# Graph network on one core: entering rows as two f32r halves, turned and summed in one matmul

## The reference

```python
x = layernorm(x + L0(x, adj))     # 5 groups of at most 25 nodes, two graph convolutions each, rows 0..24 alone change
x = layernorm(x + L1(x, adj, mask))
# L1:
A = (adj != 0)
h = x
for l in range(5):
    m = h @ weight[l]
    agg = A^T m                    # per graph, 128 x 128
    h = gru(agg, h)                # r, z: sigmoid of sums of two products; n: tanh(i_n + r * h_n)
return h * mask
```

## Time and profile before

| what | us |
|---|---|
| median of 3 runs (534.69 to 535.28) | 534.74 |
| profiled execution, its own time | 534.39 |
| its span, first to last instruction | 532.1 |
| TensorE busy | 514.9 |
| VectorE busy | 437.5 |
| ScalarE busy | 369.4 |
| GpSimd busy | 249.3 |

### The profile page before, as it was taken

One profiled execution on the slowest core, in us unless ns is written; L12 is line 12 of the kernel. 1 busy time (PEld: TensorE's weight loads), 2 busy tenths in 40 slices (PEclk: granted clock), 3 DMA queues, 4 the chain that ended last, 5 costly groups with the idle time before them and its releaser, 6 DMA issues.

```text
span 532.1 us, 8535 instructions
## 1 busy us (share of the span) xinstructions
PE 514.9 (97%) x2993; PEld 441.2 (83%) x2993; DVE 437.5 (82%) x970; ACT 369.4 (69%) x683; POOL 249.3 (47%) x299
## 2 busy tenths in 40 slices
PE   7999999999999999999999999999999999999991
PEld 6888889888888889888888889888888888888870
DVE  5479775899979877889979986688988998877886
ACT  2468665767876676787786676787785678786645
POOL 7569422458532354457633254546552245332334
PEclk9999999999999999999999999999999999999995
DMA  5967610000000000000000000000000000010002
GB/s 138 220 181 178 165 34 4 1 1 0 2 1 0 9 25 22 21 20 22 1 1 1 1 0 22 22 20 21 0 2 1 1 1 20 25 37 0 1 0 79
DMA packets 35579, 17.29 MB, mean 32 GB/s; under 512 B 4321, under 2 KB 35498, under 8 KB 35538
## 3 DMA queue, kind: packets, MB, share of 16 engines
q1 hardware_dynamic: 32233, 14.99, 10.7%
q10 hardware_dynamic: 2665, 1.54, 1.0%
q0 software_dynamic: 640, 0.22, 0.3%
HBM read 12.54 MB, written 4.19 MB: 31 GB/s over the span
## 4 chain that ended last, share of the span: by engine, by line
PE 92%; DVE 3%; SPq 2%; DMA 1%; ACT 1%; POOL 1%; issue 0%; DVEq 0%; POOLq 0%
PE p L1260 20%; PE p L1262 20%; PE p L1261 20%; PE p L1254 13%; PE p L1247 8%; PE p L1138 3%; PE p L1112 1%; PE p L1131 1%; PE p L1121 1%; DMA xt<-in_x_dram 1%; SPq L273 1%; PE p L1176 1%; SPq L268 1%; PE p L1168 1%; DVE st L930 0%; PE p L1063 0%
## 5 line engine op out<-in xcount | busy, mean ns | idle before, releaser
L486 POOL TENSOR_TENSOR dg<-hT,ng 128x512 f32<-128x512 f32 x80 | 126.1, 1576 | 255.7 <-ACT ng L706 255.6
L1260 PE MATMUL p<-ghi,wf 128*128 128x512 f32 x240 | 101.1, 421 | 0.0
L1260 PE MATMUL p<-hhi,wh 128*128 128x512 f32 x237 | 99.6, 420 | 0.0
L1262 PE MATMUL p<-ghi,wf 128*128 128x512 f32 x240 | 94.4, 393 | 0.0
L1261 PE MATMUL p<-glo,wf 128*128 128x512 f32 x240 | 93.6, 390 | 0.0
L1262 PE MATMUL p<-hhi,wh 128*128 128x512 f32 x237 | 93.1, 393 | 0.0
L1261 PE MATMUL p<-hlo,wh 128*128 128x512 f32 x237 | 92.5, 390 | 0.0
L1010 DVE SCALAR_TENSOR_TENSOR cg<-p,biasc,rg 128x512 f32<-128x512 f32 x80 | 59.9, 748 | 37.8 <-ACT rg L688 36.8
L688 ACT ACTIVATE rg<-p,gb 128x512 f32<-128x512 f32 x80 | 55.4, 692 | 34.8 <-PE p L1262 29.0
L706 ACT ACTIVATE ng<-cg,biasc 128x512 f32<-128x512 f32 x80 | 57.9, 724 | 23.1 <-DVE cg L1013 22.7
L1254 PEld LDWEIGHTS p<-an,nat 128*128 128x128 f32 x512 | 66.9, 191 | 5.1
(11 more groups left out here) (157 smaller groups left out, 846.9 us busy)
## 6 DMA issues: line engine op xcount, KB each, us to landing
xn<-in_x_dram SPq DMA_DIRECT2D x8, 512.0 KB, 4.8
an<-in_adj_dram SPq DMA_DIRECT2D x8, 512.0 KB, 7.4
out_dram<-xn SPq DMA_DIRECT2D x15, 256.0 KB, 2.3
xt<-in_x_dram SPq DMA_DIRECT2D x16, 50.0 KB
w<-in_L_gnn_W_dram ACTq DMA_DIRECT2D x1, 640.0 KB, 5.8
w<-in_L_gnn_W_dram SPq DMA_DIRECT2D x1, 640.0 KB, 4.4
zg<-in_L_gnn_weight_dram ACTq DMA_DIRECT2D x1, 320.0 KB, 3.9
xt<-in_x_dram SPq DMA_DIRECT2D x8, 36.0 KB
```

What stands on the lines that cost most here:

```text
L486: nc.gpsimd.tensor_tensor(dg[:, w.k % 2, :], hT[:, w.slot, :], ng[:, w.k % 2, :], ALU.subtract).then_inc(d_ok, 1)
L1260: MM(bank[:], w[:, 0, cols], xhi, start=start, stop=False)
L1262: return MM(bank[:], w[:, 1, cols], xhi, start=False, stop=stop)
```

## The change

- The rows of an entering visit are split into two f32r halves in er (two buffers, by visit parity): the high half by a copy (VectorE at the end of window i = 17 for the chunk's visits 0 and 1, ScalarE in windows k = 19, 20 and so on for visits 2 and 3), the low half by a subtraction on GpSimd in the window in which the visit enters, ahead of that window's dg.
- enter_and_aggregate takes the place of the four transposes and the f32 sum: per graph two f32r matmuls, weights the high and the low rows, moving 256 columns: the graph's ones and an identity that stands behind them as an's 65th block. The result holds, per graph, the masked sums and the turned state side by side; the four graphs fill banks PG and PL.
- So the entering state is there only at the end of window k. ScalarE copies the sums' high half ahead of tanh. In window k+1 it waits for glo, makes hhi, waits for the low half, and copies hT; all this stands ahead of nat and r. VectorE makes the low half (lo_entering) first of all in window k+1, ahead of the leaving rows.
- The adjacency is loaded to a buffer raw of one chunk and goes from there, as ones, to an (now f32r). SP loads a chunk's raw once the chunk before is through.
- The transposes of L0's adjacency stand at the end of window i = 2 for every chunk, and their scaling at the start of window i = 3. The neighbours' matmuls go behind the turn.
- ghi, glo have 2 buffers, nat has one.

```diff
+        er = sb("er", [128, 2, 2, SB, D], f32r)
+        both = PGL[:].rearrange("p (q o n) -> p q o n", q=SB, o=2)
+        SUMS, STATE = both[:, :, 0, :], both[:, :, 1, :]
...
+            def enter_and_aggregate(k):
+                visit = ALL_WINDOWS[k].enter
+                for q in range(SB):
+                    b = visit * SB + q
+                    moving = an[:, b:B + 1:B - b, :]
+                    MM(both[:, q], er[:, visit % 2, 0, q, :], moving, start=True, stop=False)
+                    last = MM(both[:, q], er[:, visit % 2, 1, q, :], moving, start=False, stop=True)
+                last.then_inc(G_ps, 1)
...
@@ ScalarE, window k
-                    if w.i == adjacency_in(c):
+                    if w.i == Plan.Y:
                         adjacency(c)
...
+                if coming_in(k - 1) is not None:
+                    high_state(coming_in(k - 1), None)
+                    if coming_in(k - 1) % SLOTS < 2:
+                        high_rows(coming_in(k - 1) + 2)
+                    state(coming_in(k - 1), None)
                 if w.out == "step":
                     act.wait_ge(T_ps, w.turned + 1)
...
-                if w.enter is not None and k >= 2:
-                    state(w.enter, PL)
-                    high_state(w.enter, PL)
...
+                if coming_in(k) is not None:
+                    aggregated(k + 2, None)
                 act.wait_ge(c_ok, k + 1)
@@ state and high_state, visits from 4 on
+                    act.wait_ge(glo_ok, first_window(visit) + 1)
+                    nc.scalar.copy(by_graph(hhi[:, visit % SLOTS, :]), STATE).then_inc(hi_ok, 1)
...
+                    act.wait_ge(lo_ok, first_window(visit) + 1)
+                    nc.scalar.copy(by_graph(hT[:, visit % SLOTS, :]), STATE).then_inc(hT_ok, 1)
@@ VectorE
+            def lo_entering(m):
+                dve.wait_ge(hi_ok, made(m))
+                TT(by_graph(hlo[:, m % SLOTS, :]), STATE, by_graph(hhi[:, m % SLOTS, :]), ALU.subtract).then_inc(lo_ok, 1)
+            def high_rows(visit):
+                dve.wait_ge(ln1_ok, visit + 1)
+                dve.wait_ge(G_ps, first_window(visit) - 2)
+                nc.vector.tensor_copy(er[:, visit % 2, 0], xn[:, visit * SB:(visit + 1) * SB, :]).then_inc(ehi_ok, 1)
...
-                if k >= 2 and w.enter is not None:
-                    lo_state(k + 2)
@@ GpSimd, ahead of dg in window k
+                if coming_in(w.k) is not None:
+                    low_rows(w.k)
@@ TensorE
-                if w.enter is not None and k >= 2:
-                    pe.wait_ge(ob_ok, (NG - 1) * (w.enter // SLOTS + 1))
-                    pe.wait_ge(hi_ok, k + 2)
-                    pe.wait_ge(hT_ok, w.enter)
-                    enter(w.enter, PL)
+                if c is not None and w.i == Plan.Y:
+                    neighbours(c)
...
+                if c is not None and w.i == Plan.Y - 1:
+                    pe.wait_ge(hT_ok, SLOTS * c)
+                    pe.wait_ge(lo_ok, k + 2)
+                    if c > 1:
+                        pe.wait_ge(x_ok, 2 * PACK * (c - 1))
+                    adjacency(c)
```

More of the change, by code:

```diff
@@ L143, in build @@
         xn = sb("xn", [128, B, D])
-        an = sb("an", [128, B, N])
+        an = sb("an", [128, B + 1, N], f32r)
+        raw = sb("raw", [128, CB, N])
         hT = sb("hT", [128, SLOTS, COLS])
@@ L147, in build @@
         hlo = sb("hlo", [128, SLOTS, COLS], f32r)
-        nat = sb("nat", [128, SLOTS, SB, D])
-        ghi = sb("ghi", [128, SLOTS, COLS], f32r)
-        glo = sb("glo", [128, SLOTS, COLS], f32r)
+        nat = sb("nat", [128, SB, D])
+        er = sb("er", [128, 2, 2, SB, D], f32r)
+        ghi = sb("ghi", [128, 2, COLS], f32r)
+        glo = sb("glo", [128, 2, COLS], f32r)
         rg = sb("rg", [128, 2, COLS])
@@ L210, in build, with by_graph @@
         rs2, nm2 = sb("rs2", [128, SLOTS, SB]), sb("nm2", [128, SLOTS, SB])
-        P = [ctx.enter_context(nc.psum_tensor(f"p{i}", [128, 512], f32)) for i in range(8)]
+        P = [ctx.enter_context(nc.psum_tensor(f"p{i}", [128, 512], f32)) for i in range(5)]
+        PGL = ctx.enter_context(nc.psum_tensor("pgl", [128, 2 * 512], f32))
+        P += [PGL[:, 0:512], PGL[:, 512:1024]]
+        P.append(ctx.enter_context(nc.psum_tensor("p7", [128, 512], f32)))
         PR, PH, PZ, PI, PT, PG, PL, PM = P
+        both = PGL[:].rearrange("p (q o n) -> p q o n", q=SB, o=2)
+        SUMS, STATE = both[:, :, 0, :], both[:, :, 1, :]
+        def by_graph(ap):
+            return ap.rearrange("p (q n) -> p q n", q=SB)
         WF_BANKS = (3, 4, 6, 0, 3)
@@ L283, in load_chunk, with load_graphs @@
         def load_chunk(eng, c):
-            for dst, src in ((xn, x), (an, adj)):
-                for b in (c * CB, c * CB + CB // 2):
-                    load_half(eng, dst, src, b, xa_in)
+            for b in (c * CB, c * CB + CB // 2):
+                load_half(eng, xn, x, b, xa_in)
+        def load_graphs(eng, c):
+            for at in (0, CB // 2):
+                load_half(eng, raw, adj, c * CB + at, raw_in, at)
         def group_cols(g):
@@ L330, in _ @@
                 load_half(sp, xn, x, h * CB // 2, x0_in[h])
-                load_half(sp, an, adj, h * CB // 2, a0_in[h])
+                load_half(sp, raw, adj, h * CB // 2, a0_in[h])
             sp.wait_ge(y_ps, 2)
             load_x_rows(sp, 1, range(NT), xt_in)
-            for c in range(1, CHUNKS):
-                if c >= 2:
-                    sp.wait_ge(xa_in, 64 * (c - 1))
+            load_chunk(sp, 1)
+            sp.wait_ge(a0_ok, 2)
+            sp.wait_ge(a_ok, 2)
+            load_graphs(sp, 1)
+            for c in range(2, CHUNKS):
+                sp.wait_ge(xa_in, 32 * (c - 1))
                 load_chunk(sp, c)
-                if c >= 2:
-                    load_adj_rows(sp, c, range(NT), ac_in[c])
+                load_adj_rows(sp, c, range(NT), ac_in[c])
             def leave(visit):
@@ L711, in _ @@
                     aggregated(3, PT)
-                if w.feed and k >= 2:
+                if w.feed and k >= 2 and coming_in(k) is None:
                     aggregated(k + 2, PG)
@@ L1253, in aggregate @@
                 for q in range(SB):
-                    last = MM(bank[:, q * N:(q + 1) * N], src(q), an[:, b + q, :], start=True, stop=True)
+                    last = MM(bank[:, q * N:(q + 1) * N], src(q), an[:, b + q, :].bitcast(f32), start=True, stop=True)
+                last.then_inc(G_ps, 1)
+            def enter_and_aggregate(k):
+                visit = ALL_WINDOWS[k].enter
+                for q in range(SB):
[3 more added lines that the diff above has]
+                    last = MM(both[:, q], er[:, visit % 2, 1, q, :], moving, start=False, stop=True)
                 last.then_inc(G_ps, 1)
@@ L1368, in _ @@
                     pe.wait_ge(glo_ok, 3 if k == 2 else k + 2)
+                    if coming_in(k - 1) is not None:
+                        pe.wait_ge(lo_ok, k + 2)
+                        pe.wait_ge(hT_ok, coming_in(k - 1) + 1)
                     if w.enter is not None:
                         pe.wait_ge(a_ok, w.enter - 1)
-                        aggregate(k + 2, PG, entering(w.enter))
+                        pe.wait_ge(elo_ok, w.enter - SLOTS + 1)
+                        pe.wait_ge(ob_ok, (NG - 1) * (w.enter // SLOTS + 1))
+                        pe.wait_ge(hT_ok, w.enter)
+                        enter_and_aggregate(k)
                     else:
                         pe.wait_ge(nat_ok, w.turned + 1)
[L1374 to L1377, removed]
+                        aggregate(k + 2, PG, lambda q: nat[:, q, :])
+                if c is not None and w.i == Plan.Y - 1:
+                    pe.wait_ge(hT_ok, SLOTS * c)
+                    pe.wait_ge(lo_ok, k + 2)
+                    if c > 1:
+                        pe.wait_ge(x_ok, 2 * PACK * (c - 1))
+                    adjacency(c)
             for k, bank in ((WINDOWS - 2, PT), (WINDOWS - 1, PL)):
```

85 lines of the change are left out of this document (53 added, 32 removed).

## The result

The changed kernel takes 537.53 us (median of 4 runs, 537.08 to 538.04), the kernel before 534.78 beside it: a ratio of 1.0052, 95% interval 1.004 to 1.0064. The prediction said slower, 538.9 us.

A forecast was written before the change was run, and what follows sets the result against it. TensorE, busy 97% of the span, bounds the kernel, with VectorE barely keeping pace. Entry losses of 3.2 + 1.1 = 4.3 us on the profiled 534.39 give 538.7, 539.0 for a median; stated 538.9, range 532.5 to 543.0.

The forecast's parts named there:

- TensorE's part: Entering windows on TensorE: four transposes go, eight 256-column passes at 0.92 us replace the f32 sum; 0.40 us shorter each.
- The rival with 0.23 a pass: TensorE's 256-column passes cost 0.23 us each, entering windows 6.4 us, total 541 to 543; chance 0.09.
- The cycle: Windows 18 to 22, from t1 (first gate operation, cg<-p,biasc,rg) to t1: 6.08 us against TensorE's 5.5; 6.55 in window 22.
- The walk: Chunk 1's entry, timed from window 18's start: t1 at 4.7 us, window 22's at 29.5, window 24 starting at 38.9.
- the loads and the moved neighbours of chunk 1: Chunk 1's adjacency loads waiting on SP, and its neighbours' matmuls behind the turn in window 3: priced at nothing.
- The losses: At the entries of chunks 1 and 2, 1.6 us lost each; at the last entry 1.1 us.
- The sum of 4.3: Total slowdown over the three entries, 3.2 + 1.1 = 4.3 us.
- GpSimd's twelve subtractions: Low halves of entering rows on GpSimd: 1.64 us each by one row, 1.29 by another where VectorE is quiet.
- the waits that were foretold: TensorE gaps of about 6 us: neighbours' matmuls about 1 each in windows 23, 43; nat's sums; small ones before entering sums.
- The rival "the handover stays hidden": In the entering windows only TensorE's own saving counts, -4.8 us, giving 529.9 us; chance 0.19.
- lie beside the state copy and the sigmoid and don't lengthen it: VectorE's leaving rows, 1.13 us in the entering windows, claimed not to lengthen the t1-to-t1 lap.
- estimated at 0.2 us in the prediction: First VectorE row copy waiting for GpSimd's dg under the port lock: 0.2 us later, 0.5 in the sum, left out.

The follow-up runs named there:

- experiment 11: Changed kernel with state copy and leaving rows ahead of VectorE's low half, ScalarE's row copies behind r, adjacency transposes first, VectorE's row copies early: 529.87 us, ratio 0.9903.
- experiment 1: Changed kernel with a second copy of the entering state, to an unread buffer, ahead of the copy to hT in 12 handovers: 543.54 us, ratio 1.0176.
- Experiment 4: Changed kernel with the adjacency transposes of windows 22 and 42 ahead of the masked sum, so their scaling comes earlier on ScalarE: 535.5 us, ratio 1.0015.
- experiment 10: Changed kernel with VectorE's two row copies moved from the end of window 17 to ahead of its t1: 536.84 us, ratio 1.0031.
- experiment 2: Changed kernel with ScalarE's copy of the entering state to hT behind the reset sigmoid r in windows 19 to 22: 533.81 us, ratio 0.9992.
- experiment 5: Changed kernel with ScalarE's state copy directly behind its high half, VectorE's low half waiting for it, the row copy third: 537.49 us, ratio 1.0045.
- experiment 3: Changed kernel with ScalarE's state copy behind r and VectorE's entering low half behind the leaving rows: 538.38 us, ratio 1.008.

## Why the prediction was right

- **TensorE's part.** The passes over 256 columns start 0.12 us apart (0.115 priced). Where TensorE sets the pace, in experiment 11, an entering window takes 5.56 us; before, r of windows 19 to 21 started 5.92 us apart. That is 0.36 a window against the 0.40 of the sum. The rival with 0.23 a pass is out. The Trainium skill (TensorE: Matmul & The Clock Gate, "Back-to-back issue gap") gives 0.109 for an isolated pass of that width; the trace has 0.12, and the measurement decides.
- **The cycle.** 6.08 us from t1 to t1 in the prediction; 6.04 to 6.06 measured, and 6.54 in window 22 (6.55). Every link was there, in that order. The price of the link that makes it too long is confirmed by the dose (experiment 1).
- **The walk,** from the start of window 18 (148.90): t1 of window 18 at 4.7 predicted, 153.36 - 148.90 = 4.46 measured; t1 of window 22 at 29.5 and 29.16; end of the scaling at 34.0 and 181.49 + 1.04 - 148.90 = 33.6; start of window 24 at 38.9 and 38.74. t1 of window 18 came 0.24 earlier than foretold, and the later marks 0.2 to 0.4 earlier. What the walk priced at nothing, the loads and the moved neighbours of chunk 1, cost nothing: r of window 17 starts within 0.01 us of where it did.
- **The losses.** 1.6, 1.6 and 1.1 us for the three entries; the table has 1.38, 1.54 and 1.20. Experiment 4 shows that the wait for the scaling is the path of the first two. The sum of 4.3 is 4.12 at window 64.
- **What was mis-sized** is the last step, from there to the time of a run. The last VectorE operation starts 4.08 later (532.33 against 528.25), but the span is only 3.6 longer, and around it lie 1.8 us in place of 2.3; the medians differ by 2.75. These two parts, 0.5 each, make 1.0 of the 1.4 us by which 538.9 is too high; 0.2 is the losses' own, and 0.3 the distance from the profiled run to the median, 0.35 before and 0.07 here. The first part lies in the last output transfer on ScalarE's queue, 128 KB, which landed 2.6 us after its issue in the kernel before and 2.0 in the changed one:

```profile
out_dram<-xn ACTq DMA_DIRECT2D x1, 128.0 KB, 2.6
...
out_dram<-xn ACTq DMA_DIRECT2D x1, 128.0 KB, 2.0
```

  The second part, 1.8 to 1.9 us around the span, shows in every run of every kernel made from the changed one, and 2.2 to 2.3 in every run of the kernel before. In the trace of the kernel before, queue q14, which the page calls instruction, moves a packet of 8 KB at 530.15, while this output is under way, and two more at 533.12 and 533.14, behind the end of the span (532.15). In the twelve other traces its last packet comes more than 8 us ahead of the span's end. That these packets cost the two parts isn't shown: no run moved them.
- **Small parts.** GpSimd's twelve subtractions take 1.29 to 1.42 us (1.64 and 1.29 were the rows). VectorE's row copies take 0.41 to 0.54, and the leaving rows start 0.79 behind the first of two (151.53 to 152.32), as the walk had it with 0.80. That is partly luck: undisturbed copies follow each other in 0.33 us, and the first one lost 0.13 beside GpSimd (last section). They cost 0.7 us over three entries, as experiment 10 shows. Of the waits that were foretold, those for na (0.68, about 1 foretold) and nat (0.41) show, the ones ahead of the entering sums at 0.13 to 0.22. Only that of window 18 is GpSimd's, as foretold (its subtraction ends at 153.55, the sum starts at 153.77); those of windows 20 and 21 come with the release of the banks by the state copy (experiment 2). Two of 0.24 ahead of the turns of windows 21 and 22, which wait for h, weren't foretold.
- **The rival "the handover stays hidden"** named 529.9 us for TensorE's sum alone. The changed kernel isn't that; experiment 11, with the same TensorE work, is, at 529.87. The agreement is partly luck: it has the 1.0 us less at the end of the span and around it, and a gain of 0.36, not 0.40, an entering window.
- **What the prediction did not see** is that the same sum can be had by the order of four operations. VectorE's leaving rows "lie beside the state copy and the sigmoid and don't lengthen it", it said, and that holds for this kernel by a hair: the four start at 158.07 and take 1.12, so they end at 159.19, and t1 starts at 159.40. As soon as r came earlier, they were the bound (experiments 2 and 5). And the banks had a price of their own (experiments 2 and 3).

## What to carry to other kernels

When two engines hand a tile back and forth, write down the whole lap from an operation to the same one in the next window, and compare it with the bound engine's window: here 6.08 against 5.5 told the result. Then repair the lap, not a single wait in it: an edit that takes one link out is worth only the distance to the next chain (the leaving rows, the release of the banks), and the same swap on VectorE lost 4.6 us in one order of ScalarE's copies and, with the state copy ahead, gained 6.0. A busy share won't show any of it; the chain that ended last does.

## What was not expected of the hardware

A VectorE operation with two SBUF inputs took 1.78 us beside a running GpSimd one in place of 0.68. The prediction had no row for a copy, which has one input, and left such a wait out of its sum. The copies wait too. In the changed kernel GpSimd's dg runs from 150.49 to 151.78, and the first row copy starts at 151.53; in experiment 10 no such subtraction runs beside the copies. GpSimd's and VectorE's timelines, and the copies' line in both kernels (ns min/median/max), the changed one first:

```profile
150.49 1.29 POOL L526 TENSOR_TENSOR dg<-hT,ng 128x512 f32<-128x512 f32 x1 [2.18 <-ACT ng L762]
...
151.53 0.87 DVE L977 CAST er<-xn 128x512 fp32r<-128x512 f32 x2
...
L977 DVE CAST er<-xn x6: 411/475/541, 151.5 to 403.1; 128x512 fp32r<-128x512 f32 x6
...
L977 DVE CAST er<-xn x6: 414/414/415, 146.9 to 397.9; 128x512 fp32r<-128x512 f32 x6
```

In each of the three entries the first copy of the pair, the one that starts beside dg, takes 0.54 us and the second 0.41; in experiment 10 both take 0.41. So the first one lost 0.13, some 0.4 us over three entries, while dg kept its usual 1.29. The two rows fit one account, an estimate from these figures: the operation stands still until about 0.13 us before the end of dg's record and then takes its usual time. From 151.53 to 151.65, and 0.41 more, is 152.07, where the copy ends; from 162.22 to 163.32 (dg ends at 163.45 there), and 0.68 more, is 164.00, where the two-input operation ends. The rule of the Trainium skill (SBUF — State Buffer, "SBUF: two separate sides") by which the first copy would wait for dg, estimated at 0.2 us in the prediction, is borne out by these rows for a copy that rounds to f32r, at 0.13.
